# First attention: the key-side product in the bank of the small third product, turned blocks and corrections in two banks by turns

## The reference

```python
scores = jnp.einsum('bhqd,bhkd->bhqk', Q, K) * scale
c2p = take_along_axis(einsum('bhqd,shd->bhqs', Q, pos_key) * scale, clip(rel + 64, 0, 127))
p2c = take_along_axis(einsum('bhkd,shd->bhks', K, pos_query) * scale, clip(-rel + 64, 0, 127))
scores = scores + c2p + swapaxes(p2c, -1, -2)
probs = softmax(scores); ctx = probs @ V
```

## Time and profile before

| | |
|---|---|
| median of 3 runs | 2113.69 us (2112.2 to 2116.16) |
| profiled execution | 2112.18 us, span 2110.4 us |
| TensorE, VectorE, ScalarE busy over the span | 82%, 70%, 70% |
| first attention, steady part (200 to 946 us) | PE 92%, DVE 85%, ACT 87% of 746 us |
| granted clock of TensorE in that part | 1.00 |

### The profile page before, as it was taken

One profiled execution on the slowest core, in us unless ns is written; L12 is line 12 of the kernel. 1 busy time (PEld: TensorE's weight loads), 2 busy tenths in 40 slices (PEclk: granted clock), 3 DMA queues, 4 the chain that ended last, 5 costly groups with the idle time before them and its releaser, 6 DMA issues. The chain is left out here.

```text
span 2110.4 us, 44034 instructions
## 1 busy us (share of the span) xinstructions
PE 1724.6 (82%) x11670; PEld 1044.7 (50%) x11670; DVE 1468.4 (70%) x3508; ACT 1466.8 (70%) x2584; POOL 79.4 (4%) x102
## 2 busy tenths in 40 slices
PE   2316999999999999983861799999999994999998
PEld 1203555555555555552540465565556552545544
DVE  2635888888888888872983788888888882423422
ACT  2304888888888888881872799999999993223222
POOL 0000000000000000000540000000000000000000
PEclk9656999999999999996985899999999997999999
DMA  2966999998899999955687777777777763100100
GB/s 71 353 217 195 271 270 276 275 269 271 271 274 277 270 271 276 272 163 153 206 299 257 200 210 213 213 213 211 212 212 213 211 180 100 35 20 22 37 5 10
DMA packets 419996, 420.89 MB, mean 199 GB/s; under 512 B 36016, under 2 KB 325320, under 8 KB 419808
## 3 DMA queue, kind: packets, MB, share of 16 engines
q1 hardware_dynamic: 419936, 420.19, 67.1%
HBM read 232.47 MB, written 187.00 MB: 199 GB/s over the span
## 5 line engine op out<-in xcount | busy, mean ns | idle before, releaser
L817 ACT ACTIVATE a_prob<-bank,a_negmax 128x512 f32<-128x512 f32 x1024 | 734.6, 717 | 51.3 <-DVE a_negmax L749 49.6
L749 DVE TENSOR_REDUCE a_negmax<-bank 128x1 f32<-128x512 f32 x1024 | 699.5, 683 | 0.2 <-issue 0.2
L631 PE MATMUL bank<-a_ident,a_prob 128*128 128x128 f32 x4096 | 644.1, 280 | 60.1 <-ACT a_probt L824 50.8
L824 ACT COPY a_probt<-bank 128x512 f32<-128x512 f32 x1024 | 616.2, 602 | 87.4 <-PE bank L631 73.7
L631 PEld LDWEIGHTS bank<-a_ident,a_prob 128*128 128x128 f32 x4096 | 449.5, 141 | 181.9 <-issue 76.5
L741 DVE TENSOR_TENSOR bank<-bank,a_band 128x128 f32<-128x128 f32 (+3 forms) x1024 | 350.2, 342 | 80.1 <-PE bank L612 68.4
L610 PE MATMUL bank<-a_stks 65*128 65x192 bf16 (+7 forms) x1024 | 323.0, 316 | 10.5 <-ACT a_prob L817 10.2
L644 PE MATMUL bank<-a_probt,a_vs 128*32 128x512 f32 x2048 | 272.4, 606 | 15.0 <-ACT a_probt L824 15.0
L610 PEld LDWEIGHTS bank<-a_stks 65*128 65x128 bf16 (+1 forms) x1024 | 100.1, 98 | 231.8 <-ACT a_prob L817 202.4
L729 DVE COPY_PREDICATED bank<-a_mask,bank 128x128 f32<-128x128 uint32 (+1 forms) x512 | 139.4, 272 | 107.2 <-PE bank L616 107.1
L612 PE MATMUL bank<-a_stks 65*128 65x320 bf16 (+5 forms) x768 | 201.1, 262 | 0.0
(11 more groups left out here) (169 smaller groups left out, 1567.9 us busy)
## 6 DMA issues: line engine op xcount, KB each, us to landing
a_band<-shear_b SPq DMA_DIRECT2D x128, 512.0 KB, 4.4
shear_a<-a_keyside SPq DMA_DIRECT2D x128, 256.0 KB, 3.4
a_sheared<-shear_a SPq DMA_DIRECT2D x128, 256.0 KB, 4.4
shear_b<-a_corr SPq DMA_DIRECT2D x128, 256.0 KB, 4.4
shear_e<-a_corr SPq DMA_DIRECT2D x128, 256.0 KB, 2.3
a_band<-shear_e SPq DMA_DIRECT2D x128, 256.0 KB, 3.4
a_stks<-stack SPq DMA_DIRECT2D x128, 192.0 KB, 4.5
a_stks<-stack SPq DMA_DIRECT2D x128, 144.0 KB, 2.9
```

The lines of the kernel that those rows point to most:

```text
L631: last = pe.transpose(turned_bank[k][:, n * 128:(n + 1) * 128], prob[h.slot % 2][:, n, k * 128:(k + 1) * 128], ident[:, :])
L749: v.tensor_reduce(negmax[h.slot % 2][:, n:n + 1], score[:, :], AX.X, ALU.max, negate=True).then_inc(maxed, 1)
L817: nc.scalar.activation(prob[h.slot % 2][:, n, :], score[:, :], ACT.Exp, bias=negmax[h.slot % 2][:, n:n + 1]).then_inc(exped, 1)
L824: nc.scalar.copy(probt[h.slot][:, k, :], turned_bank[k][:, :]).then_inc(copied, 1)
```

## The change

The key-side product goes to the bank `other`, which the third products use. It waits for the patch of the tile before (`fixed`), and the third product of the next tile (tile 0, k = 2) waits for `key_copied`. `key_out` moves one instruction up on VectorE, before finish(3). The two banks 5 and 6 then take the turned blocks and the correction strictly by turns, five uses per head, so which bank comes first swings with the head. `turn(h, 2)` now waits for the copy of block 0, `turn(h, 3)` for that of block 1, and `turn(h, 3)` no longer waits for `key_out`.

```diff
-                turned_bank = [bank[5], bank[6], bank[6], bank[5]] if rel else [bank[5], bank[6]] * 2
-                key_bank, corr_bank = bank[5], bank[6] if rel else bank[4]
+                swing = bank[5:7]
+                key_bank = other
...
+                def turned_bank(h, k):
+                    return swing[(h.slot + k) % 2] if rel else swing[k % 2]
+
+                def corr_bank(h):
+                    return swing[h.slot % 2] if rel else other
...
                         if rel:
                             pe.wait_ge(fixed, BASE + tile)
+                            if keys_out is not None:
+                                pe.wait_ge(key_copied, BASE + keys_out)
                             a, e = fix_cols(n)
                             last = pe.matmul(other[:, 0:e - a], k[:, qhi, q], k[:, khi, a:e], start=True, stop=True)
...
                         if rel and k == 1:
                             pe.wait_ge(corr_copied, BASE + made(h.n + corr_ahead))
-                        elif rel and k == 3:
-                            pe.wait_ge(key_copied, BASE + made(h.n + KEY_AHEAD + 1))
+                        elif rel:
+                            pe.wait_ge(copied, BASE + 4 * h.n + max(k - 1, 0))
                         else:
-                            pe.wait_ge(copied, BASE + 4 * h.n + (k if rel else k - 1))
+                            pe.wait_ge(copied, BASE + 4 * h.n + k - 1)
...
-                                score_tile(pe, *ahead(i, j, k, score_ahead))
+                                score_tile(pe, *ahead(i, j, k, score_ahead), made(own.n + KEY_AHEAD + 1) if rel and k == 2 else None)
...
                             if rel and k == 1 and left >= KEY_AHEAD:
-                                pe.wait_ge(copied, BASE + 4 * own.n + 1)
+                                pe.wait_ge(fixed, BASE + 4 * own.n + 1 + score_ahead + 1)
                                 key_side(pe, Head(i, j + KEY_AHEAD))
...
                                     row_max(v, *ahead(i, j, k, score_ahead - 1))
+                                if rel and k == 1 and left >= KEY_AHEAD:
+                                    key_out(v, Head(i, j + KEY_AHEAD))
                                 if rel and left >= (k + score_ahead) // NT:
                                     finish(v, *ahead(i, j, k, score_ahead))
...
-                                if rel and k == 1 and left >= KEY_AHEAD:
-                                    key_out(v, Head(i, j + KEY_AHEAD))
```

More of the change, by code:

```diff
@@ L595, in _, with score_tile @@
                         sp.wait_ge(out_written, BASE + 16 * NG)
-                    def score_tile(pe, h, n):
+                    def score_tile(pe, h, n, keys_out=None):
                         tile, k = 4 * h.n + n, stk[h.slot]
@@ L625, in turn @@
                             pe.wait_ge(corr_copied, BASE + made(h.n + corr_ahead))
-                        elif rel and k == 3:
-                            pe.wait_ge(key_copied, BASE + made(h.n + KEY_AHEAD + 1))
+                        elif rel:
+                            pe.wait_ge(copied, BASE + 4 * h.n + max(k - 1, 0))
                         else:
-                            pe.wait_ge(copied, BASE + 4 * h.n + (k if rel else k - 1))
+                            pe.wait_ge(copied, BASE + 4 * h.n + k - 1)
                         for n in range(NT):
-                            last = pe.transpose(turned_bank[k][:, n * 128:(n + 1) * 128],
+                            last = pe.transpose(turned_bank(h, k)[:, n * 128:(n + 1) * 128],
                                                 prob[h.slot % 2][:, n, k * 128:(k + 1) * 128], ident[:, :])
@@ L657, in correction @@
                             q = slice(128 * n, 128 * n + 128)
-                            pe.matmul(corr_bank[:, q], sheared[h.slot % 4][:, q], ident[:, :], is_transpose=True, start=True, stop=False)
-                            last = pe.matmul(corr_bank[:, q], stk[h.slot][:, QLO, q], tab[h.slot][:, REL:2 * REL], start=False, stop=True)
+                            pe.matmul(corr_bank(h)[:, q], sheared[h.slot % 4][:, q], ident[:, :], is_transpose=True, start=True, stop=False)
+                            last = pe.matmul(corr_bank(h)[:, q], stk[h.slot][:, QLO, q], tab[h.slot][:, REL:2 * REL], start=False, stop=True)
                         last.then_inc(corr_mm, 1)
@@ L667, in edge @@
                             q = slice(128 * n, 128 * n + 128)
-                            last = pe.matmul(corr_bank[:, q], stk[h.slot][:, EDGE, q], edges[:, :], start=True, stop=True)
+                            last = pe.matmul(corr_bank(h)[:, q], stk[h.slot][:, EDGE, q], edges[:, :], start=True, stop=True)
                         last.then_inc(corr_mm, 1)
@@ L753, in edge_out @@
                         v.wait_ge(e_written[h.slot % 2], BASE + 16 * h.use(2))
-                        v.tensor_copy(corr[h.slot % 2][:, :, :], corr_bank[:, :].rearrange("p (n r) -> p n r", n=NT)).then_inc(corr_copied, 1)
+                        v.tensor_copy(corr[h.slot % 2][:, :, :], corr_bank(h)[:, :].rearrange("p (n r) -> p n r", n=NT)).then_inc(corr_copied, 1)
                     def key_out(v, h):
@@ L823, in copy_turned @@
                             act.wait_ge(pv_mm, BASE + 16 * (h.use(GROUP) - vslots + 1))
-                        nc.scalar.copy(probt[h.slot][:, k, :], turned_bank[k][:, :]).then_inc(copied, 1)
+                        nc.scalar.copy(probt[h.slot][:, k, :], turned_bank(h, k)[:, :]).then_inc(copied, 1)
                     def group_out(act, h):
@@ L834, in corr_out @@
                         act.wait_ge(b_written, BASE + 16 * (h.n - 1))
-                        nc.scalar.copy(corr[h.slot % 2][:, :, :], corr_bank[:, :].rearrange("p (n r) -> p n r", n=NT)).then_inc(corr_copied, 1)
+                        nc.scalar.copy(corr[h.slot % 2][:, :, :], corr_bank(h)[:, :].rearrange("p (n r) -> p n r", n=NT)).then_inc(corr_copied, 1)
                     @block.scalar
```

## The result

The changed kernel takes 2156.38 us (median of 4 runs, 2152.96 to 2157.53) against 2112.94 us (4 runs, 2112.19 to 2116.16) for the kernel before: ratio 1.020, 95% interval 1.0182 to 1.0218. It is 43.4 us slower. The forecast was 2149 us, with a range of 2135 to 2163.

A forecast was written before the change was run, and what follows sets the result against it. The prediction took a 5.95 us loop per head across VectorE, ScalarE and TensorE as the bound. It added 0.26 for the held third product and 0.03 for a second wait: 122 x 0.29 = 35 us, forecast 2149 us, range 2135 to 2163.

The forecast's parts named there:

- What bounds the kernel: A closed loop over VectorE, ScalarE and TensorE, mix(3) to mix(3), sets the head at 5.95 us; no engine is full.
- The waits that go: turn(2) no longer waits for copy_turned(h, 1); TensorE idled 0.18 there, but off the loop, so counted 0.
- The third product waits for key_out: Tile 0's third product starts 0.07 after key_out ends, mix(0) 0.37 after that: mix(0) 0.26 later per head.
- No stall before key_out: On VectorE, key_out takes finish(3)'s slot at 508.93, 0.02 after its data are there, so no stall was counted.
- Two waits on one instruction: The third product carries waits for `fixed` and `key_copied`; cost between 0 and 0.08, taken as 0.03.
- Sum: 0.26 and 0.03 make 0.29 a head; 122 x 0.29 = 35 us, giving 2149 us, 1.7% slower.
- upper bound of 0.40: High end per head: 0.26, 0.08 for the second wait and 0.06 on the correction path; 49 us, 2163.
- The signs: Profile after: VectorE waits before mix(0), 1.86 to 1.92 after mix(3); key_out at 0.74; head 6.2 to 6.3 us.
- Correction path: Rival: turned block 2, its copy and the correction come late, TensorE's own queue holds turn(0); 2162 us, chance 0.2.
- Faster: Rival: turn(2)'s bank wait, on a second loop through turn(2) and the copies, sets the head; 2092 us, chance 0.04.
- no change: Rival: the new order is hidden, with key-side product and copy leaving mix(0) where it is; 2114 us, chance 0.04.
- Clock: Rival: new TensorE gaps before the third product bring the granted clock down to 0.50; 2256 us, chance 0.02.

The follow-up runs named there:

- e2: Changed kernel with key_out put back behind finish(3) on VectorE: 2172.23 us, ratio 1.0287.
- e4: Changed kernel with the key-side product's wait for the patch written last, behind its two waits for loads: 2152.97 us, ratio 1.0189.
- e7: Changed kernel with key_out copying 256 of 512 columns past the prologue: 2126.46 us, ratio 1.0057.
- e8: Changed kernel with the key-side product making 256 of 512 columns past the prologue, the copy whole: 2145.21 us, ratio 1.0154.
- e1: Kernel before with only key_out moved ahead of finish(3) on VectorE, banks and waits as before: 2111.52 against 2112.12 us, ratio 1.000.
- e3: Changed kernel with turned blocks and correction on the old fixed banks, turn(2) again waiting for copy_turned(1): 2157.10 us, ratio 1.0213.
- e11: Kernel before with ScalarE's copy of the weighted sums moved ahead of copy_turned(1) in the first attention: 2110.77 against 2110.51 us, ratio 0.9996.
- e5: Changed kernel with the key-side product right behind turn(0), its copy behind finish(2), tile 3's third product waiting for it: 2128.41 us, ratio 1.0067.
- e9: e5 with the table load one step earlier in SP's queue: 2126.49 us, ratio 1.0081.
- e10: e9 with ScalarE's copy of the weighted sums ahead of copy_turned(1) in the first attention: 2118.68 us, ratio 1.0045.

## Why the prediction held, point by point

- *What bounds the kernel.* Right. The loop of 5.95 us was the pace-setter: a step of it that was moved by 0.18 (e2), 0.19 (e4), 0.27 (e7) or 0.08 (e8) moved the head by the same within 0.01, and what was changed outside it (e1, e3, e11) moved nothing.
- *The waits that go count nothing.* Right, by e3. The second loop that the last heads showed is real too: without a key side the head went from 5.61 to 5.36 with the alternation.
- *The third product waits for key_out.* Right in place and mechanism. The 0.07 after the copy was 0.06, and the 0.37 to mix(0) was 0.38.
- *No stall before key_out.* This term was mis-sized. I took 0.04 from the end of the product to the copy, from a stretch in which the granted clock was 0.50 and the product took 0.63. Here it was 502.70 - 502.17 - 0.39 = 0.14, and the head got 0.08 that I had as nothing. e8 gives the 0.08 back. Another hand-over from TensorE to VectorE, the 0.15 from the third product's end to mix(3), would have been the better measure. It does not hang on the clock: at 0.50 it is 184.93 - 184.47 - 0.31 = 0.15 as well.

```profile
184.47 0.31 PE L616 MATMUL bank<-a_stks 65*128 65x128 bf16 x1
...
184.93 0.30 DVE L729 COPY_PREDICATED bank<-a_mask,bank 128x128 f32<-128x128 uint32 x1 [5.46 <-PE bank L616]
```

  Why the row of the key side at the lower clock has 0.04 stays open; the ends of matmuls are modelled in these rows.
- *Two waits on one instruction, 0.03.* The third product paid nothing: 0.06 from the copy's end, and 0.07 before with one wait. In the built program it carries only the wait for the copy, the last to come. The key-side product's new wait cost 0.19 in two slots of eight, a mean of 0.05, a cost that the prediction had nowhere (e4).
- *Sum.* 0.26 + 0.09 = 0.35 in an ordinary head (0.08 for the stall, 0.01 in the hand-overs) and 0.53 in two of eight, mean 0.40 and not 0.29. That makes the 43 us, for 35 forecast. The mean lies at the upper bound of 0.40, and that the bound held is luck in part: it was added up from a second wait of 0.08 and a correction path of 0.06, neither of which came about, and the stall and the separate wait, about as large, were not in it.
- *The signs.* VectorE waits before mix(0), as forecast, and turn(2) no longer waits for ScalarE. The sizes were short: key_out at 0.82 and 1.00 for 0.74, mix(0) at 1.95 and 2.13 for 1.86 to 1.92, the head at 6.30 and 6.48 for 6.2 to 6.3.
- *Rivals.* Correction path: no, but narrowly. turn(0) came 0.73 after the start of copy 3, as before (0.72), so ScalarE released it; TensorE's own queue was done at 505.98, only 0.08 before turn(0), and in some slots not before its start. Faster, no change: no. Clock: no in this kernel; it stayed at 1.00 through a gap of 0.67 before each held product. By "TensorE: Matmul & The Clock Gate" of the Trainium skill, section "A second HAM failure mode: psum-queue depth-cycling", frequent short idle spells between groups of matmuls made the clock of another kernel oscillate; this trace does not show it. The clock did fall in e5, e9 and e10, in heads of over 8 us, so that this rival was not an idle one.

## What to carry to other kernels

Before giving two uses one buffer, write down how long each holds it, first write to last read with the hand-overs, and lay this in the timeline of the loop that sets the pace. Here mix(3) leaves the bank at 0.23, and the key side keeps the next third product out until 1.57 (503.45 - 501.88): 1.34 us. To leave mix(0) at 1.60, that product could start no later than 1.60 - 0.38 = 1.22, which leaves 0.99. The difference is the 0.35 that the ordinary head grew by. Then ask for the place with the most idle time on the reading engine, and only then for the order of banks. And if a second limit lies close behind the first, as the late band seems to here, shortening the first gives little: look at it before counting the gain.

## What was not expected of the hardware

- A semaphore wait that the built program puts on an instruction ahead of the product it protects delayed that product by 0.19 us (0.48 and not 0.29 after the start of the patch); written last in the source, the same wait cost nothing (e4). The profile called this time "issue".
- The gap from the key-side product's printed end to the start of its copy was 0.14 at a granted clock of 1.00 and 0.04 at 0.50, while the gap from a third product to its patch was 0.15 at both.
- The clock stayed at 1.00 with a gap of 0.67 us on TensorE in every head of 6.3 us, while in e10 it fell to 0.50 in three heads in which TensorE had stood 1.14, 0.79 and 0.81 us ahead of a third product.
- A copy of 128 x 256 took 0.42 us and one of 128 x 512 0.69: half the columns save 0.27, not half the time. The expectation of e7 had worked this out from the additions of 192 and 256 columns.
